# Looser waits at both ends, reordered weight preparation, and a shorter power of two in a fused Mamba-and-FFN kernel

## The chip, the cores and the metric

The kernel runs on one core of a Trainium2 chip. Its time is the device time of one execution in microseconds (us); the kernel before takes 1848.21 us, the median of three runs (1847.84 to 1850.84). Everything below comes from one profiled execution of it, which took 1849.32 us, of which 1847.5 us are the span that the trace covers.

## The reference, cut to what matters

For an input x of 2 x 2048 rows of 512 numbers the reference computes `x + attn(xn) + ffn(xn)`, where `xn` is the layer norm of x.

- `attn` is a Mamba-2 layer: `xn @ in_proj_w` gives z, x, B, C and dt; x goes through a causal convolution of four taps and a silu; a chunked state-space product with decays follows; the result is normed, scaled by `norm_scale` and `silu(z)` and multiplied by `out_proj_w`.
- `ffn` is a gated layer between Walsh-Hadamard transforms: `fwht(xn * SU_ug)`, then the products with `W_up` and `W_gate` (2048 x 512 each), `silu(gate) * up`, `fwht(. * SU_dp)`, and the product with `W_down` (512 x 2048), with scale vectors per row.

The transforms act on the activations in the reference; the kernel moves them onto the weights, once, ahead of the blocks.

## The kernel before, in words

The program has two parts. The **preparation** turns the weights into pairs of 16-bit tiles (a high part and a low rest) with power-of-two scales. The **blocks** then work through 16 blocks of 256 rows; every product with weights is three 16-bit products (high with high, high with low, low with high).

Every engine follows a list of step names written out by hand, in the preparation (`PREP_PE`, `PREP_ACT`, `PREP_DVE`, `PREP_SP`, lines 80 to 101) and in the blocks (`PE_STEPS` and the others). Each engine works its list strictly in order and waits in it on semaphores.

Steps of the preparation:

- **Loads (SP's list).** `nat0` to `nat7` are the eight groups of 512 rows of w_up and w_gate (1 MB each; `nat0` is loaded from ScalarE's queue at the very start). `dn0` and `dn2` are the two halves of w_down (2 MB each), `in` is in_proj (two loads of 2 MB and one of 288 KB), `wo1` is out_proj for its norms (2 MB), and `wo2` is out_proj again for its own preparation. `nat2` and later wait until group n-2 has been squared and mixed (lines 362 to 366).
- **Group of up or gate.** VectorE adds and subtracts halves (`bb`, lines 509 and 510, into `mixed`); ScalarE sums squares of the group's rows (`sq`, line 422); TensorE sums them over the partitions (`fs`, line 693, one product over four columns into bank 7), and VectorE (`fs`, lines 588 to 595) reduces the four, takes a power of two above the root (`power_above`) and its inverse, and scales the sign vector with it into `su_scale`. Four units per group follow: TensorE transposes four tiles (`T`, line 717), ScalarE copies them from the bank (`T`, line 437, into `wt`), TensorE multiplies with the Hadamard matrix (`H`, lines 728 and 729), ScalarE stores the high part with the group's scale (`H`, line 449), and VectorE stores the low rest (`H`, line 624). There are 32 such units, and 16 more of w_down.
- **w_down.** ScalarE scales its four rows of tiles (`dsc`, line 460) and squares them (`dsq`, line 464); VectorE mixes it in eight butterfly steps (`db`, lines 509 and 510 with 2048 columns; the digits are stage and half); T32 to T47 wait for all eight.
- **in_proj.** ScalarE squares pieces (`nq`, line 432), TensorE sums them (`nb`, line 700), VectorE takes maxima (`nb`), finds the scales (`ws`), and both store the pair (`wi`, lines 454 and 666).
- **Peaks (`pk`).** VectorE finds all remaining scales in some 10 us of small dependent steps with two exchanges with TensorE (lines 514 to 575). ScalarE's `pk` is only a wait for them. After it come out_proj (`wo`) and the units of w_down.
- **The first block's input.** VectorE norms it (`lna`, `lnb`, `lnc`), ScalarE and VectorE split it (`xh`, `xl`), and SP turns it with four DMA transposes (`turn_x`).

At the end of the preparation each of the five engines counts up `prepared`, and all wait there for 5 (lines 829, 894, 1016, 1154 and 1342). VectorE then drains, releases the ring's banks (line 1343) and clears the running state. TensorE's `bank` waits, for each ring product, until the bank's prior content has been read; for the first block this is line 1343's release.

In the blocks TensorE's list holds the FFN's gate and up products (`F0` to `F15`), its down products (`D`), the products of the state space (`xp`, `qk`, `cs`, `G`, `int`, `itr`, `st`, `z`) and out_proj (`O0`, `O1`); `D` and `O` collect in banks 6 and 7. All products go through the helper at line 910. SP's list loads the next block's input (`xin`), turns v, y and the next x (`td`, `yd`, `xd`), loads the residual (`res`) and stores the block before (`store`). In the last block `xin` loads block 0 again, and it is normed and turned for nothing. After the last block VectorE sums both halves (`final_sum`, line 1338) and SP stores 512 KB in one transfer (line 885).

Of the kernel before, what the change touches and what calls it, by code (L numbers as in the profile page):

```python
# [80 lines left out]
fs0 T0 T1 T2 H0 H1 T3 nb0 fs1 T4 H2 T5 H3 T6 T7 H4 H5 H6 T8 H7 T9 nb1 fs2 H8 T10 T11 nb2 H9 nb3 H10 H11 fs3  # L81
T12 nb4 T13 nb5 T14 H12 H13 T15 T16 fs4 T17 H14 H15 T18 T19 H16 H17 T20 H18 H19 T21 fs5 H20 H21 T22 T23 T24
H22 fs6 H23 T25 T26 H24 T27 H25 fs7 T28 H26 H27 T29 pk H28 T30 H29 T31 H30 H31 T32 T33 H32 T34 H33 T35 H34 T36
H35 T37 T38 H36 H37 T39 T40 H38 T41 H39 H40 T42 T43 H41 T44 T45 H42 H43 T46 H44 T47 H45 H46 H47
""".split()
PREP_ACT = """
sq0 nq0 dsc0 T0 T1 dsc1 sq1 T2 H0 dsc2 T3 H1 dsc3 dsq0 dsq1 T4 T5 H2 dsq2 dsq3 H3 H4 T6 T7 sq2 nq1 T8 T9 H5 H6
nq2 nq3 H7 T10 T11 sq3 H8 nq4 H9 nq5 H10 T12 T13 sq4 H11 H12 T14 T15 wi0 wi1 H13 T16 T17 H14 H15 wi2 wi3 T18
T19 sq5 H16 H17 T20 H18 T21 H19 sq6 T22 T23 H20 sq7 H21 T24 T25 H22 H23 H24 H25 T26 T27 H26 T28 H27 T29 T30
H28 H29 pk T31 wo0 wo1 wo2 H30 wo3 H31 wo4 wo5 T32 T33 wo6 T34 wo7 T35 H32 T36 H33 H34 T37 H35 H36 T38 H37 T39  # L90
T40 H38 T41 H39 T42 H40 T43 xh0 xh1 H41 T44 H42 T45 H43 T46 H44 T47 H45 H46 H47
""".split()
PREP_DVE = """
bb0 bb1 fs0 db00 H0 bb2 fs1 H1 nb0 db01 bb3 H2 db10 H3 H4 db11 fs2 nb1 H5 bb4 H6 nb2 H7 db20 nb3 fs3 H8 nb4 H9
H10 nb5 ws H11 bb5 H12 fs4 wi0 wi1 H13 H14 H15 wi2 wi3 db21 H16 H17 H18 H19 bb6 fs5 bb7 H20 db30 H21 fs6 H22
H23 H24 H25 fs7 pk H26 H27 db31 wo0 wo1 H28 H29 H30 wo2 H31 wo3 wo4 wo5 wo6 wo7 H32 H33 H34 H35 H36 lna H37
lnb lnc H38 H39 xl0 xl1 H40 H41 H42 H43 H44 H45 H46 H47
""".split()
PREP_SP = """
wo1 dn0 nat1 dn2 nat2 nat3 in nat4 nat5 nat6 nat7 wo2  # L100
# [40 lines left out]
def program(nc, u, in_w, conv_w, conv_b, a_log, dt_bias, d_param, norm_scale, out_w,  # L141
# [10 lines left out]
    with ctx:  # L152
# [115 lines left out]
        with ExitStack() as prep:  # L268
# [135 lines left out]
            def _(act):  # L404
# [9 lines left out]
                for step in PREP_ACT:  # L414
# [23 lines left out]
                    elif k == "H":  # L438
# [7 lines left out]
                        else:  # L446
                            a = n - UG_UNITS
                            dst, sc = wd[:, a, 0, :], down_store[:, a:a + 1]
# [17 lines left out]
                    elif k == "pk":  # L466
                        act.wait_ge(all_scales, 1)
                    elif k == "wo":
# [6 lines left out]
            def _(dve):  # L475
# [36 lines left out]
                def peaks():  # L512
# [7 lines left out]
                    power_above(rowpw[:, :], pw[:, :])  # L520
                    nc.vector.tensor_tensor(rowpw[:, :].rearrange("p (g t) -> p g t", g=8), cols[:, WS_UG:WS_UG + 32].rearrange("p (g t) -> p g t", g=8),
# [56 lines left out]
                for step in PREP_DVE:  # L578
# [100 lines left out]
            def _(pe):  # L679
# [7 lines left out]
                for step in PREP_PE:  # L687
                    k, n = parse(step)
                    if k == "fs":
# [3 lines left out]
                        nc.tensor.matmul(banks[7][:, 4 * n:4 * n + 4], ones[:, :], nsq[:, 4 * n:4 * n + 4], start=True, stop=True).then_inc(group_summed, 1)  # L693
# [126 lines left out]

        def position(step):
            return ring[RING.index(step) % BANKS]
# [5 lines left out]
        def _(sp):  # L828
            sp.wait_ge(prepared, 5)

            def body(i, following, first=False):
                for s in SP_STEPS:
                    k, at = kind(s), index(s)
                    if k == "store":
# [15 lines left out]
                    elif k == "xin":  # L850
# [3 lines left out]
                        sp.dma_start(xin[:, :, :], x_v[following]).then_inc(x_loaded, 16)  # L854
# [27 lines left out]
            for i in range(NBLOCKS):  # L882
                body(i, (i + 1) % NBLOCKS, first=i == 0)
            sp.wait_ge(out_ready, NBLOCKS * NT)
# [498 lines left out]
```

## Time and profile before

| | us |
|---|---|
| median of three runs | 1848.21 |
| profiled execution | 1849.32 |
| its span | 1847.5 |
| start of TensorE's first block product | 162.34 |
| TensorE busy, from 270 to 1740 us | 1470.00 |
| last product starts | 1836.87 |
| store leaves | 1844.23 |

Times in the rows are microseconds from the start of the span. PE is TensorE, PEld its weight loads, DVE VectorE, ACT ScalarE, POOL GpSimd, SPq and ACTq the queues from which DMAs are issued. "L509" is line 509 of the kernel. A bracket behind an instruction tells how long its engine was idle before it and whose event ended that; `<-issue` means that no wait was seen. A busy TensorE is not a TensorE at its peak, as its products are pipelined.

### The profile page before, as it was taken

How to read it: one execution, taken by the hardware profiler on the slowest of the kernel's cores; microseconds unless marked ns; L12 is line 12 of the kernel's file. 1: busy time of each engine (PE TensorE's matmuls, PEld its weight loads, DVE VectorE, ACT ScalarE, POOL GpSimd, SP SyncE). 2: the span in 40 equal slices, each digit the busy share in tenths (PEclk: the TensorE clock that was granted, in tenths of full speed). 3: DMA queues.
4: the chain of work that ended last, by engine and by line, in shares of the span. 5: the costliest groups of instructions: out<-in, count | busy, mean ns of one | idle time of the engine just before them, and what ended most of it. 6: DMA issues, size and time to landing. Idle time of an engine off the chain costs nothing.

```text
span 1847.5 us, 37420 instructions
## 1 busy us (share of the span) xinstructions
PE 1793.8 (97%) x13746; PEld 1241.9 (67%) x13746; DVE 1391.4 (75%) x2859; ACT 1223.8 (66%) x2582; POOL 306.4 (17%) x270
## 2 busy tenths in 40 slices
PE   4878999999999999999999999999999999999998
PEld 2336767676766768676766758677666757676675
DVE  6987867869586877868586877958676776858686
ACT  7967848576574848666584847666584857657483
POOL 0000212203030212203021221203021220303021
PEclk9999999999999999999999999999999999999999
DMA  8111223121312222131312322131322213121222
GB/s 326 69 69 47 58 58 81 32 81 39 81 47 61 78 47 76 41 79 41 89 47 58 81 44 76 36 78 47 85 53 58 81 34 74 43 81 47 64 75 58
DMA packets 217581, 125.74 MB, mean 68 GB/s; under 512 B 179662, under 2 KB 180790, under 8 KB 216886
## 3 DMA queue, kind: packets, MB, share of 16 engines
q1 hardware_dynamic: 216870, 122.30, 25.0%
q8 instruction: 109, 1.79, 0.4%
q10 hardware_dynamic: 528, 1.05, 0.2%
q14 instruction: 74, 0.61, 0.1%
HBM read 72.18 MB, written 8.65 MB: 44 GB/s over the span
## 4 chain that ended last, share of the span: by engine, by line
PE 90%; DVE 5%; DMA 1%; ACT 1%; issue 1%; SPq 1%; DVEq 1%; ACTq 0%
PE bank L910 88%; DMA big<-in_L_ffn_W_down_dram 1%; DVE wug L624 1%; DVE wi L666 1%; PE bank L728 1%; PE bank L729 0%; DVE big L509 0%; ACT big L460 0%; DVE wo L675 0%; SPq L873 0%; PE bank L717 0%; DVE wd L509 0%; DVE big L510 0%; ACT wi L464 0%; PE bank L732 0%
## 5 line engine op out<-in xcount | busy, mean ns | idle before, releaser
L910 PE MATMUL bank<-pair,wug 128*128 128x256 f16 x6144 | 699.8, 273 | 0.0
L910 PEld LDWEIGHTS bank<-pair,wug 128*128 128x128 f16 x6144 | 596.3, 98 | 90.3 <-issue 3.4
L910 PE MATMUL bank<-wd,h 128*128 128x512 f16 x1536 | 360.3, 379 | 0.0
L1183 POOL TENSOR_TENSOR state<-state,dec 128x512 f32<-128x512 f32 x64 | 84.2, 1325 | 1066.2 <-ACT neg L1098 805.4
L910 PEld LDWEIGHTS bank<-wd,h 128*128 128x128 f16 x1536 | 149.1, 98 | 160.5 <-DVE h L1241 0.2
L1230 DVE SCALAR_TENSOR_TENSOR pair<-pair,conv 128x256 f32<-128x256 f32 x384 | 193.2, 548 | 78.8 <-ACT pair L1046 68.9
L910 PE MATMUL bank<-wi,pair 128*128 128x512 f16 (+1 forms) x1152 | 201.6, 330 | 3.1 <-DVEq L1343 3.1
L910 PE MATMUL bank<-pair,wi 128*128 128x256 f16 x1536 | 172.9, 273 | 0.0
L1112 ACT ACTIVATE Mx<-Mx,cs_own 128x128 f32<-128x128 f32 x512 | 162.2, 388 | 8.2 <-DMA Mx<-cs_rows 7.6
L910 PEld LDWEIGHTS bank<-wi,pair 128*128 128x128 f16 x1152 | 101.5, 99 | 98.0 <-issue 3.9
L910 PEld LDWEIGHTS bank<-pair,wi 128*128 128x128 f16 x1536 | 149.9, 98 | 16.9
L1171 POOL TENSOR_TENSOR pair<-v 128x512 f32<-128x512 f16 x64 | 81.7, 1276 | 431.0 <-DMA v<-pair 385.9
L1263 DVE TENSOR_TENSOR Mx<-Mx,Gm 128x512 f32<-128x512 f32 x128 | 97.8, 764 | 32.7 <-ACT Mx L1116 23.5
L1061 ACT ACTIVATE pair<-bank,gate_scale 128x256 f32<-128x256 f32 x128 | 60.3, 471 | 91.5 <-PE bank L910 67.6
L1090 ACT ACTIVATE stateK<-state 128x512 f16<-128x512 f32 x64 | 39.7, 620 | 90.7 <-DVE state L1295 90.7
L1295 DVE SCALAR_TENSOR_TENSOR state<-bank,state 128x512 f32<-128x512 f32 x64 | 44.0, 688 | 73.5 <-PE bank L910 73.4
L1061 ACT ACTIVATE tg<-bank,gate_scale 128x256 f32<-128x256 f32 x128 | 59.8, 467 | 49.4 <-PE bank L910 48.5
L1237 DVE SCALAR_TENSOR_TENSOR tg<-tg,h_scale,bank 128x256 f32<-128x256 f32 x128 | 61.0, 476 | 37.7 <-ACT tg L1061 34.2
L1116 ACT ACTIVATE Mx<-Mx 128x512 f32<-128x512 f32 x128 | 80.6, 630 | 8.1
L910 PE MATMUL bank<-wo,Mx 128*128 128x512 f16 x384 | 85.5, 379 | 0.0
L910 PE MATMUL bank<-wo,yT 128*128 128x512 f16 x384 | 85.5, 379 | 0.0
L1268 DVE TENSOR_TENSOR Mx<-Mx 128x512 f16<-128x512 f32 x96 | 75.2, 783 | 12.7 <-ACT Mx L1127 10.6
(253 smaller groups left out, 2715.9 us busy)
## 6 DMA issues: line engine op xcount, KB each, us to landing
Mx<-cs_rows SPq DMA_DIRECT2D x128, 256.0 KB, 3.7
pair<-in_L_attn_u_dram SPq DMA_DIRECT2D x17, 512.0 KB, 3.6
Mx<-in_L_attn_u_dram SPq DMA_DIRECT2D x16, 512.0 KB, 3.8
out_dram<-Mx SPq DMA_DIRECT2D x16, 512.0 KB, 2.8
big<-in_L_ffn_W_down_dram SPq DMA_DIRECT2D x2, 2048.0 KB, 18.1
wug<-in_L_attn_in_proj_w_dram SPq DMA_DIRECT2D x2, 2048.0 KB, 13.4
pair<-in_L_ffn_W_gate_dram SPq DMA_DIRECT2D x4, 1024.0 KB, 5.3
pair<-in_L_ffn_W_up_dram SPq DMA_DIRECT2D x3, 1024.0 KB, 16.9
```

What stands on the lines that cost most here:

```text
L910: ins = nc.tensor.matmul(out, lhsT, rhs, start=first and n == 0, stop=last and n == len(pairs) - 1)
L1061: nc.scalar.activation(tg[c % 2][:, :], ug[c % 2][:, 0:TB], ACT.Silu, scale=gate_scale[:, c:c + 1]).then_inc(gate_ready, 1)
L1090: nc.scalar.activation(stateK[:, hf * 512:(hf + 1) * 512], state[:, hf * 512:(hf + 1) * 512], ACT.Copy, scale=1.0 / LOW).then_inc(state_hi ...
L1112: nc.scalar.activation(M[q][:, n, :], M[q][:, n, :], ACT.Relu, scale=-1.0, bias=cs_own[:, c, 4 * q + n:4 * q + n + 1])
L1116: nc.scalar.activation(M[q][:, :, :], M[q][:, :, :], ACT.Exp, scale=-1.0).then_inc(M_exp, 1)
L1171: pool.tensor_tensor(by_tile(vd[:, :]), v16[:, 4 * hf:4 * hf + 4, c, 0, :], v16[:, 4 * hf:4 * hf + 4, c, 1, :], ALU.add)
L1183: pool.tensor_tensor(half, half, bcast(dec3[:, 2, c, 8 * hf:8 * hf + 8], HD), ALU.mult).then_inc(state_faded, 1)
L1230: ins = nc.vector.scalar_tensor_tensor(cv[n % 2][:, c, :], x[:, c, j:j + TB], conv[:, CX * j + t:CX * j + t + 1], cv[n % 2][:, c, :], ALU. ...
L1237: nc.vector.scalar_tensor_tensor(tg[c % 2][:, :], tg[c % 2][:, :], h_scale[:, c:c + 1], ug[c % 2][:, TB:2 * TB], ALU.mult, ALU.mult).then_ ...
L1263: nc.vector.tensor_tensor(M[q][:, :, :], M[q][:, :, :], Gm[:, c, :].unsqueeze(1).to_broadcast([P, 4, P]), ALU.mult).then_inc(M_whole, 1)
L1268: nc.vector.tensor_tensor(M_lo[q], M[q][:, :, :], M_hi[q], ALU.subtract).then_inc(M_ready, 1)
L1295: nc.vector.scalar_tensor_tensor(half, o[:, :], 1.0 / PEAK, half, ALU.mult, ALU.add).then_inc(dve_emptied, 1)
```

## The change

- A group's power of two: TensorE adds the four columns itself (four products over one column into the same cell of bank 7), and VectorE shifts the exponent by 24 right and 23 left, takes the inverse as a multiply and add on the bits, and scales the signs. The power itself is taken back from the inverse for all groups at once in the peaks.
- New lists for TensorE, ScalarE, VectorE and SP. SP's now loads `dn0 nat1 dn2 nat2` ahead of `wo1` and `in`.
- ScalarE's `pk` wait goes; the wait for all scales stands in `wo` and in the units of w_down.
- TensorE waits at the start of the blocks for the split in_proj and the last copy (`wi_split`, `wt_copied`) in place of `prepared`; in the first block `bank` waits for the stores of the units only for banks 2 and 3, F0 and F1 wait for them, and `O` waits for the split out_proj.
- The last block loads, norms, splits and turns no further input. The last store is two stores, one for each half, and the final sum waits for the last down product only for the half that it closes.

```diff
 PREP_PE = """
...
+T0 T1 H0 T2 T3 H1 fs0 fs1 T4 H2 H3 T5 T6 H4 T7 H5 H6 T8 H7 T9 nb0 nb1 nb2 H8 T10 fs2 H9 T11 nb3 T12 H10 T13
+H11 nb4 T14 fs3 nb5 H12 T15 H13 T16 H14 H15 fs4 T17 T18 T19 H16 H17 T20 H18 H19 T21 fs5 T22 H20 H21 T23 T24
+H22 H23 T25 fs6 T26 H24 H25 T27 fs7 T28 H26 H27 T29 pk H28 H29 T30 T31 T32 H30 H31 T33 H32 T34 H33 T35 H34 T36
+T37 H35 H36 T38 T39 H37 T40 H38 T41 H39 H40 T42 H41 T43 T44 H42 T45 H43 H44 T46 H45 T47 H46 H47
 PREP_ACT = """
...
+T0 sq0 T1 dsc0 dsc1 dsq0 sq1 H0 T2 T3 H1 dsq1 dsc2 H2 dsc3 T4 T5 dsq2 H3 dsq3 T6 T7 H4 nq0 H5 nq1 T8 T9 nq2
+sq2 H6 nq3 nq4 H7 T10 H8 T11 H9 nq5 sq3 H10 T12 T13 H11 sq4 wi0 T14 T15 wi1 H12 H13 H14 T16 H15 T17 wi2 wi3
+T18 T19 sq5 H16 T20 T21 H17 H18 H19 H20 T22 T23 sq6 H21 T24 H22 T25 sq7 H23 H24 T26 T27 H25 H26 T28 T29 H27
+H28 H29 T30 T31 wo0 wo1 wo2 wo3 H30 wo4 T32 T33 wo5 wo6 T34 wo7 H31 T35 H32 T36 H33 H34 T37 T38 H35 H36 T39
+H37 T40 H38 T41 H39 T42 xh0 H40 T43 xh1 H41 T44 T45 H42 H43 T46 T47 H44 H45 H46 H47
 PREP_DVE = """
...
+bb0 db00 fs0 bb1 fs1 bb2 H0 H1 H2 db01 H3 db10 db11 nb0 bb3 H4 nb1 db20 H5 fs2 H6 nb2 db21 nb3 H7 H8 H9 bb4
+nb4 H10 fs3 nb5 ws bb5 H11 wi0 wi1 H12 H13 H14 fs4 H15 wi2 wi3 bb6 H16 fs5 H17 H18 H19 db30 bb7 H20 H21 fs6
+db31 H22 H23 H24 H25 fs7 pk H26 H27 wo0 H28 H29 wo1 wo2 H30 wo3 wo4 wo5 wo6 wo7 H31 H32 H33 H34 lna H35 H36
+H37 lnb lnc H38 xl0 H39 H40 xl1 H41 H42 H43 H44 H45 H46 H47
 PREP_SP = """
-wo1 dn0 nat1 dn2 nat2 nat3 in nat4 nat5 nat6 nat7 wo2
+dn0 nat1 dn2 nat2 wo1 in nat3 nat4 nat5 nat6 nat7 wo2
...
                     elif k == "fs":
-                        nc.vector.reduce_sum(fsq[:, g], banks[7][:, 4 * n:4 * n + 4], AX_X)
-                        dve.drain()
-                        power_above(fsq[:, g], fpw[:, g])
-                        inverse_power(fpw[:, g], fsq[:, g])
+                        nc.vector.tensor_scalar(fpw[:, g].bitcast(I32), banks[7][:, g].bitcast(I32), 24, 23, ALU.logical_shift_right, ALU.logical_shift_left)
+                        dve.drain()
+                        nc.vector.tensor_scalar(fsq[:, g].bitcast(I32), fpw[:, g].bitcast(I32), -1.0, float((254 - 65) << 23), ALU.mult, ALU.add)
+                        dve.drain()
...
-                        nc.tensor.matmul(banks[7][:, 4 * n:4 * n + 4], ones[:, :], nsq[:, 4 * n:4 * n + 4], start=True, stop=True).then_inc(group_summed, 1)
+                        for t in range(4):
+                            ins = nc.tensor.matmul(banks[7][:, n:n + 1], ones[:, :], nsq[:, 4 * n + t:4 * n + t + 1], start=t == 0, stop=t == 3)
+                        ins.then_inc(group_summed, 1)
...
-            sp.wait_ge(out_ready, NBLOCKS * NT)
-            sp.dma_start(out_v[NBLOCKS - 1], res[:, :, :]).then_inc(out_stored, 16)
...
+            for j in range(NT):
+                sp.wait_ge(out_ready, (NBLOCKS - 1) * NT + j + 1)
+                sp.dma_start(out_v[NBLOCKS - 1][:, j, :], res[:, j, :]).then_inc(out_stored, 16)
...
-            pe.wait_ge(prepared, 5)
+            pe.wait_ge(wi_split, 1)
+            pe.wait_ge(wt_copied, UNITS)
 
             def bank(i, s):
...
+                if ago > i:
+                    if RING.index(s) % BANKS >= 2:
+                        pe.wait_ge(hw_stored, UNITS)
+                    return position(s)
...
                     elif k == "F":
-                        pe.wait_ge(h_whole, (i + 1) * KF + c - 1)
+                        if i == 0 and c < 2:
+                            pe.wait_ge(hw_stored, UNITS)
+                        else:
+                            pe.wait_ge(h_whole, (i + 1) * KF + c - 1)
...
-                dve.wait_ge(h_used, (i + 1) * KF)
                 for j in range(NT):
+                    if down_closes(j):
+                        dve.wait_ge(h_used, (i + 1) * KF)
```

## Rows read from the trace of the kernel before

**Rows 1.** Windows: length, busy time (instructions) of each engine, granted clock, DMA share, GB/s.
```profile
22.28:160.77 138.49, 110.50 (x389) 55.65 (x389) 126.92 (x245) 112.88 (x208) 0.00 (x0) 0.96 0.31 108
8.90:107.90 99.00, 71.12 (x238) 35.86 (x239) 80.88 (x127) 87.83 (x166) 0.00 (x0) 0.95 0.46 175
...
162.34:165.06 2.72, 2.72 (x24) 2.72 (x25) 1.59 (x4) 0.00 (x0) 0.00 (x0) 0.50 0.02 6
270.00:1740.00 1470.00, 1470.00 (x11694) 1035.66 (x11692) 1101.72 (x2275) 962.27 (x2058) 265.37 (x224) 1.00 0.24 61
```

**Rows 2.** Waits of VectorE from 22.28 to 161 us: total, times, longest.
```profile
DVE wo L509 <- DMA pair<-in_L_ffn_W_up_dram: 13.5, 1, 13.5
...
DVE big L509 <- ACT wi L464: 0.3, 1, 0.3
```

**Rows 3.** Timeline of the opening: start, duration, engine, line, operation.
```profile
14.61 5.00 ACT L432 ACTIVATE wi<-wi,cols 128x512 bf16<-128x512 f32 x8 [2.63 <-DMA wi<-n_L_attn_out_proj_w_dram]
19.68 2.00 ACT L460 ACTIVATE big<-big,down_scale 128x2048 f32<-128x2048 f32 x1
...
22.28 1.22 DVE L509 TENSOR_TENSOR wo<-pair 128x1024 f32<-128x1024 f32 x1 [13.47 <-DMA pair<-in_L_ffn_W_up_dram]
...
26.04 2.29 DVE L509 TENSOR_TENSOR wd<-big 128x2048 f32<-128x2048 f32 x1
```

**Rows 4.** Timeline of one group's sum and power of two.
```profile
30.56 0.36 PE L693 MATMUL bank<-nsq,ones 128*128 128x4 f32 x2 [0.30 <-PE bank L700]
...
33.38 0.15 DVE L591 TENSOR_REDUCE fsq<-bank 128x1 f32<-128x4 f32 x1
...
34.53 0.23 DVE L595 TENSOR_SCALAR su_scale<-cols,fsq 128x4 f32<-128x4 f32 x1
```

**Rows 5.** Timeline: the last group's power of two begins.
```profile
115.71 0.15 DVE L591 TENSOR_REDUCE fsq<-bank 128x1 f32<-128x4 f32 x1
```

**Rows 6.** Timeline of the change from the preparation to the blocks.
```profile
157.65 1.26 SPq L266 DMA_TRANSPOSE pair<-pair  x1
...
158.63 2.14 DVE L624 SCALAR_TENSOR_TENSOR wd<-bank,down_store,wd 128x512 f16<-128x512 f32 x3 [0.55 <-ACT wd L449]
...
162.34 3.02 PE L910 MATMUL bank<-wi,pair 128*128 128x144 f16 x24 [3.09 <-DVEq L1343]
...
165.40 0.48 DVE L1201 TENSOR_SCALAR raw<-bank,scal 128x256 f32<-128x256 f32 x1 [1.09 <-PE bank L910]
...
169.41 0.18 DVE L1220 TENSOR_SCALAR pair<-pair 128x32 f32<-128x32 f32 x1
...
173.06 0.27 PE L954 MATMUL bank<-ident,kq 128*128 128x128 f32 x1
```

**Rows 7.** Timeline: two Hadamard products of TensorE after idle stretches.
```profile
97.44 2.08 PE L728 MATMUL bank<-wt,had 128*128 128x512 f32 x2 [3.51 <-DVE wug L624]
...
128.31 1.12 PE L728 MATMUL bank<-wt,had 128*128 128x512 f32 x2 [2.06 <-DVE wug L624]
```

**Rows 8.** Timeline of the end.
```profile
1833.11 1.90 SPq L265 DMA_TRANSPOSE pair<-pair  x1
...
1836.87 5.34 PE L910 MATMUL bank<-wo,Mx 128*128 128x512 f16 x24
...
1839.00 0.58 SPq L857 DMA_DIRECT2D Mx<-in_L_attn_u_dram  x1
1842.80 1.41 DVE L1338 SCALAR_TENSOR_TENSOR Mx<-bank,scal,Mx 128x512 f32<-128x512 f32 x2 [4.95 <-DMA Mx<-in_L_attn_u_dram]
1844.23 0.39 SPq L885 DMA_DIRECT2D out_dram<-Mx  x1
```

**Rows 9.** DMA issues of the whole span: count, KB each, median us to landing.
```profile
out_dram<-Mx SPq DMA_DIRECT2D x16, 512.0 KB, 2.8
...
pair<-pair SPq DMA_TRANSPOSE x68, 2.5
pair<-in_L_ffn_W_up_dram ACTq DMA_DIRECT2D x1, 1024.0 KB, 5.4
```

More of the change, by code:

```diff
@@ L447, in _ @@
                             a = n - UG_UNITS
+                            act.wait_ge(all_scales, 1)
                             dst, sc = wd[:, a, 0, :], down_store[:, a:a + 1]
@@ L520, in peaks @@
                     power_above(rowpw[:, :], pw[:, :])
+                    inverse_power(fsq[:, :], fpw[:, :])
                     nc.vector.tensor_tensor(rowpw[:, :].rearrange("p (g t) -> p g t", g=8), cols[:, WS_UG:WS_UG + 32].rearrange("p (g t) -> p g t", g=8),
@@ L819, in number, with down_closes @@
             return at[0] if len(at) == 1 else 10 * at[0] + at[1]
+        def down_closes(j):
+            return PE_STEPS.index(f"D{KF - 1}") > PE_STEPS.index(f"O{j}")
         def position(step):
@@ L829, in _, with body @@
             sp.wait_ge(prepared, 5)
-            def body(i, following, first=False):
+            def body(i, first=False, last=False):
                 for s in SP_STEPS:
                     k, at = kind(s), index(s)
+                    if last and k in ("xin", "xd"):
+                        continue
                     if k == "store":
@@ L853, in body @@
                         sp.wait_ge(v_turned[3], (i + 1) * 2 * 16)
-                        sp.dma_start(xin[:, :, :], x_v[following]).then_inc(x_loaded, 16)
+                        sp.dma_start(xin[:, :, :], x_v[i + 1]).then_inc(x_loaded, 16)
                     elif k == "res":
@@ L882, in _ @@
             for i in range(NBLOCKS):
-                body(i, (i + 1) % NBLOCKS, first=i == 0)
-            sp.wait_ge(out_ready, NBLOCKS * NT)
-            sp.dma_start(out_v[NBLOCKS - 1], res[:, :, :]).then_inc(out_stored, 16)
-            sp.wait_ge(x_loaded, 16 * (NBLOCKS + 1))
-            sp.wait_ge(out_stored, 16 * (NBLOCKS + 1))
-            sp.wait_ge(xT_loaded, 4 * 16 * (NBLOCKS + 1))
+                body(i, first=i == 0, last=i == NBLOCKS - 1)
+            for j in range(NT):
+                sp.wait_ge(out_ready, (NBLOCKS - 1) * NT + j + 1)
+                sp.dma_start(out_v[NBLOCKS - 1][:, j, :], res[:, j, :]).then_inc(out_stored, 16)
+            sp.wait_ge(out_stored, 16 * (NBLOCKS + 2))
         @block.tensor
@@ L901, in bank @@
                 return position(s)
-            def down_closes(j):
-                return PE_STEPS.index(f"D{KF - 1}") > PE_STEPS.index(f"O{j}")
             def products(out, pairs, first=True, last=True):
@@ L1003, in body @@
                         pe.wait_ge(yT_loaded[c], (i + 1) * 4 * 16)
+                        pe.wait_ge(wo_split, CX)
                         products(acc[c][:, :], [pq for a in range(CX) for pq in three(lambda u: yT[c][:, a, u, :], lambda u: wo[:, a, u, :])],
@@ L1143, in body @@
                         nc.scalar.activation(by_tile(y_hi[c][hf]), y[c][hf], ACT.Copy).then_inc(y_high, 1)
-                    elif k == "xh":
+                    elif k == "xh" and i < NBLOCKS - 1:
                         act.wait_ge(dve_emptied, (i + 1) * NR_DVE + emptied("itr11"))
@@ L1320, in body @@
                         nc.vector.tensor_tensor(by_tile(y_lo[c][hf]), y[c][hf], by_tile(y_hi[c][hf]), ALU.subtract).then_inc(y_split, 1)
-                    elif k == "xl":
+                    elif k == "xl" and i < NBLOCKS - 1:
                         low_xn(dve, i, at[0])
-                    elif k == "lna":
+                    elif k == "lna" and i < NBLOCKS - 1:
                         norm_sums(dve, i)
-                    elif k == "lnb":
+                    elif k == "lnb" and i < NBLOCKS - 1:
                         norm_root(dve)
-                    elif k == "lnc":
+                    elif k == "lnc" and i < NBLOCKS - 1:
                         norm_apply()
```

16 lines of the change are left out of this document (1 added, 15 removed).

## The prediction

> **What bounds the kernel now.** I read the windows by stage first. From 270 to 1740 us TensorE is busy 1470.00 of 1470.00 us at full granted clock [rows 1]: there the blocks cost what TensorE's products cost, and the change takes none of them out. So only two places can move: the preparation, before TensorE's first block product at 162.34 us [rows 6], and the tail after its last product, which ends at 1836.87 + 5.34 = 1842.21 us [rows 8].
>
> Next the waits of VectorE from its second group butterfly (22.28 us) to its last low half (158.63 + 2.14 = 160.77 us) [rows 3, 6]. The first row is 13.5 us for a load of w_up, which ends at 22.28; it and the last row are shown, and the six after the first sum to 3.8 us [rows 2]. So in those 138.5 us VectorE's queue stands still for 3.8 us and is taken for 134.7 us (busy 126.92, the rest are drains between dependent steps) [rows 1]. VectorE bounds the preparation; ScalarE (112.88) and TensorE (110.50) have room over the whole, but up to its last square sum at 107.9 us ScalarE is busy 87.83 of 99 us [rows 1]. It is the next bound.
>
> **The change, part by part.** The sum is made against the profiled execution: 1849.32 us, of which 1847.5 are span. It lies 1.1 us over the median of 1848.21; I take the gains off either.
>
> *The power of two in three steps.* Now a group's chain is six dependent VectorE steps; the first five start 0.23 us apart (33.38 to 34.53) [rows 4]. Reduce, add and one shift go: 3 x 0.23 = 0.69 us, for 8 groups 5.5 us. One more inverse, with its drain, comes into the peaks: 0.25 us. Net 5.3 us less on the bounding queue. TensorE gives back: the one product over 4 columns, two passes in 0.36 us [rows 4], becomes four such products over one column, so at most +1.08 us a group, 8.6 us in all. TensorE is free 28 of 138.5 us [rows 1], and the group chain (TensorE +1.08 at most, VectorE -0.69) grows by 0.4 us at most, so I cost it at nothing; with TensorE's room gone it costs up to 8.6.
>
> *New load order.* Now out_proj goes first and lands at 14.6, where ScalarE starts on it; the first half of w_down, queued behind it, lands at 19.68, and VectorE's first down butterfly comes at 26.04 [rows 3]. After, that half of w_down has the place of out_proj, and is as large (2 MB), so it lands near 14.6. ScalarE scales two rows (2.00 each [rows 3]) and VectorE begins its long run with that butterfly at about 14.6 + 4.0 = 18.6 us, not with w_up at 22.28. The next w_up group then arrives behind 3 MB and is hidden by the butterfly's 4.5 us. out_proj and in_proj come later by what passed them (3 MB, near 8 us), but ScalarE now takes their squares after the fourth row of w_down has been squared, at about 40 and 46 us in a walk through its new order; some 14 MB at the opening's pace are in at about 39. That cover is some 6 us; if it is gone, each us late is a us on ScalarE's early run.
>
> *New orders.* From 18.6 us VectorE has 134.7 - 5.5 + 0.25 = 129.4 us to do: its end would be 148.0 with no wait, 151.8 with the 3.8 us of now. Walking through the three lists with the durations of now, I find two new waits: about 1.7 us before the second half of the first down butterfly (ScalarE reaches the fourth row's scaling only at 33 us, behind a group's square sums), and 0 to 2 us of ScalarE's early run, which ends near 108 us as now. The last group's power is then found at about 113 us instead of 115.71 [rows 5], with a 4.4 us butterfly that came behind it already done ahead of it. So I take 5.5 us of waits: VectorE ends at 153.5, 7.3 us earlier. Bounds: 2 us of waits (most of today's gone, 150.0) and 10 (ScalarE or TensorE feeds it late, 158). The last unit steps (TensorE 13 transposes and products after VectorE's 31st low half) come out at about the same 153 us, so less than 150 is hard to get. ScalarE's wait for all scales moves to steps that need them: it was 4 us of idle ScalarE in a stretch where VectorE worked without pause; nothing.
>
> *TensorE's first wait.* Today TensorE starts 162.34 - 160.77 = 1.57 us after VectorE's last step: VectorE drains, joins the barrier, drains again and releases the banks. After, only the copies of the weights, the split in_proj and the turned x hold it. x's last transpose was issued at 157.65 and lands 2.5 us later [rows 6, 9], 160.15; in the new order VectorE's second low half of x stands one step nearer the end, so x lands at about VectorE's end. I take TensorE's start 0.2 us after it: 1.4 us gained (bounds 0.5 and 2.5). The banks of the last units are guarded in the third ring product and the first F, 3 to 5 us on, when VectorE is done. What is late next is VectorE itself: it still clears the state after the barrier, ready 3.55 us after its end (at 164.31, then 1.09 of wait for TensorE), and its chain to the decay inputs ends 4.2 us after the first bank is read (165.40 to 169.41 + 0.18), so at +7.8; TensorE asks for them 10.7 us after its start (173.06) [rows 6], or 9.5 with a fast first product. Covered by about 2 us.
>
> *The clock at the start.* The first product takes 2.72 us at granted 0.50, after 3.09 us of idle TensorE [rows 1, 6]. After a gap of 2.06 us a Hadamard product of two passes took 1.12, after one of 3.51 us 2.08 [rows 7]. The new gap is 1.5 (TensorE leaves before VectorE) + 0.2 = 1.7 us, nearer the first: then 24 products of 144 columns at full clock take near 1.5, saving 1.2 us (bounds 0 and 1.3). The Trainium skill (TensorE: Matmul & The Clock Gate, Part 1: The HAM clock gate) says that half rate is the idle state and that recent activity releases it; by it any restart from idle could be slow, and the sum would be 1.2 us higher. The trace agrees with it only for the longer gap.
>
> *The tail.* The last block skips the next block's load, norm and four transposes, so SP asks for the residual near 1833, where the first of those four stands now, not at 1839.00; it lands near 1837, under it TensorE's last product (1842.21). Today the residual lands at 1842.80, two sums run to 1844.21, and the store leaves at 1844.23 [rows 8]. After, the first half is summed and stored under the last product (its wait, D15, ends at 1837); the second starts at about 1842.27 and takes 0.73, its store leaves at 1843.03: 1.2 us gained. A store of 512 KB lands in 2.8 us; loads of 512 KB and 1 MB (3.8, 5.4 [rows 8, 9]) differ by 1.6, so half the bytes save at most 0.8 and at least 0: I take 0.4. Tail 1.6 us. What VectorE and ScalarE skip in the last block lies under TensorE and gives nothing, as do the added wait in O and the weaker wait in the final sum of the inner blocks.
>
> Sum: 7.3 + 1.4 + 1.2 + 1.6 = 11.5 us. Profiled 1837.8; median **1836.7**.
>
> **Rivals.**
> *A, VectorE unhindered.* Its waits shrink to 2 us (150.0), start and tail at their good ends: 10.8 + 2.5 + 1.2 + 2.0 = 16.5, 1831.7. For it: VectorE waits only 3.8 us now [rows 2]. Against: the unit chain at the end, and ScalarE's early run.
> *B, ScalarE and TensorE set the pace.* ScalarE gains only about 1 us by its fourth group's squares in my walk; if it and the unit chain hold VectorE to 10 us of waits, its end is 158: 2.8 + 1.4 + 1.2 + 1.6 = 7.0, 1841.2.
> *C, slower: TensorE falls to half clock and becomes the bound.* Its Hadamard product is 1.9 times as long cold [rows 7]. The 110.50 busy us of now were at a mean clock of 0.96 [rows 1]; at 0.75 they would be 141, with up to 8.6 us of extra sums some 149. With 19 us before its steady run TensorE ends near 168 and the body starts 6 us later than now, less 1.6 in the tail: about 1852. It becomes the bound at a mean clock under about 0.84 (126 + 8.6 + 19 = 153.6) and eats the whole gain under about 0.77. For it: six more passes per group, and a wait on VectorE of 3.51 us occurs now. Against: earlier data, fewer idle stretches.
> *D, the loosened start doesn't do it.* x, or something that this trace does not show, holds TensorE's start as now, and cold: 7.3 + 1.6 = 8.9, 1839.3.
>
> **How the numbers follow.** The forecast 0.50, A 0.15, B 0.20, C 0.05, D 0.10. Range 1831 to 1844: from A's end to beyond B; C and the poorer part of B stay out. The measurement tells 0.2% (3.7 us) from no change. Faster than 1844.5: the forecast, A, D and most of B, 0.87; within 0.2%: the tail of B with D added, 0.08; slower: C, 0.05.
>
> **What would show it.** The profile after should have: a VectorE group chain of three steps, near 0.6 us from first start to the next work; the first down butterfly near 18.6; VectorE's last low half near 153.5, with waits of about 5.5 us between; TensorE's first block product less than 0.5 us after that, in 1.5 us at clock near 1.0; no wait of TensorE before the transposes of q and k; the second half's sum 0.1 us behind the last product and the span's end about 4 us behind it instead of 5.3. A down load landing past 17 us, an end of VectorE past 158, or TensorE's clock under 0.8 in the preparation would make the prediction wrong.

## The result and the profile after

The changed kernel takes 1838.43 us (median of six runs, 1837.27 to 1839.65), the kernel before beside it 1849.01 (six runs, 1847.84 to 1850.84). The ratio is 0.9941, with a 95% interval of 0.9931 to 0.9951: some 11 us less. The profiled execution took 1837.27 us, of which 1835.6 are span; before it was 1847.5, so 11.9 us are to be found in the traces. It is the fastest of the six, 1.2 us under their median, and the medians differ by 10.6 us, so some 1 us of the 11.9 may be scatter. Four executions among the experiments below, two of them of the kernel before, took 4.9 to 10.8 ms and are left out of every figure.

The timeline of the opening, after (start, duration, engine, line, operation):

```profile
14.04 3.88 ACT L461 ACTIVATE big<-big,down_scale 128x2048 f32<-128x2048 f32 x2
...
17.96 2.29 DVE L509 TENSOR_TENSOR wd<-big 128x2048 f32<-128x2048 f32 x1 [9.15 <-ACT big L461]
...
21.04 0.95 PE L695 MATMUL bank<-nsq,ones 128*128 128x1 f32 x8
...
22.37 0.15 DVE L592 TENSOR_SCALAR fpw<-bank 128x1 int32<-128x1 int32 x1
22.60 0.15 DVE L594 TENSOR_SCALAR fsq<-fpw 128x1 int32<-128x1 int32 x1
22.83 0.23 DVE L596 TENSOR_SCALAR su_scale<-cols,fsq 128x4 f32<-128x4 f32 x1
22.97 1.22 DVE L509 TENSOR_TENSOR wo<-pair 128x1024 f32<-128x1024 f32 x1
```

ScalarE scales w_down at 14.04 where it squared out_proj before, and VectorE's first down butterfly comes at 17.96 instead of 26.04 [rows 3]. A group's power takes 0.60 us of VectorE (22.37 to 22.97). TensorE's sum now takes eight passes, 0.95 us, where two took 0.36 [rows 4]: some 0.6 us more a group.

Windows after (columns as in [rows 1]): VectorE's stretch, the first block product, and from the second product to the last product's end.

```profile
17.96:155.24 137.28, 112.95 (x460) 60.87 (x459) 123.69 (x222) 115.31 (x214) 0.00 (x0) 0.96 0.35 120
...
153.76:155.27 1.51, 1.51 (x24) 1.51 (x25) 1.48 (x3) 0.46 (x1) 0.00 (x0) 1.00 0.00 0
155.27:1832.31 1677.04, 1677.04 (x13323) 1180.61 (x13320) 1255.41 (x2578) 1097.50 (x2349) 302.24 (x256) 1.00 0.24 61
```

The body, 1677.04 us, is what it was: before, its second product began at 165.18 and its last one ended at 1842.21, 1677.03 apart. All of the gain lies at the two ends. The first product runs at granted clock 1.00 in 1.51 us, against 0.50 and 2.72 [rows 1]. (The granted clock is given as a share of full speed: 1.00 is TensorE's level of 2.4 GHz, 0.50 that of 1.2 GHz, and a value between them is a stretch with both.)

Waits of VectorE after, from its first down butterfly on (total, times, longest; the first row's 9.2 lies ahead of it):

```profile
DVE wd L509 <- ACT big L461: 10.3, 2, 9.2
DVE wd L625 <- ACT wd L450: 2.4, 4, 1.2
DVE fpw L592 <- PE bank L695: 1.2, 1, 1.2
DVE wug L625 <- ACT wug L450: 0.6, 1, 0.6
```

With the 1.1 us left of the first row and six rows of 0.3 to 0.6 that are not shown, these make about 7.7 us. The largest are the units of w_down at the end and one group sum on which VectorE stood.

The hand-over to the blocks, after:

```profile
147.93 0.68 DVE L255 SCALAR_TENSOR_TENSOR pair<-pair 128x512 f16<-128x512 f32 x1
...
149.88 1.41 DVE L625 SCALAR_TENSOR_TENSOR wd<-bank,down_store,wd 128x512 f16<-128x512 f32 x2 [0.60 <-ACT wd L450]
...
151.19 1.26 SPq L266 DMA_TRANSPOSE pair<-pair  x1
...
152.51 2.73 DVE L625 SCALAR_TENSOR_TENSOR wd<-bank,down_store,wd 128x512 f16<-128x512 f32 x4 [1.23 <-ACT wd L450]
153.76 1.67 PE L919 MATMUL bank<-wi,pair 128*128 128x144 f16 x24 [0.62 <-DMA pair<-pair]
...
162.88 0.18 DVE L1233 TENSOR_SCALAR pair<-pair 128x32 f32<-128x32 f32 x1
...
163.13 0.31 PE L966 MATMUL bank<-ident,kq 128*128 128x128 f32 x1
```

TensorE starts at 153.76, after 0.62 us of idleness that the last transpose of x ended (issued at 151.19), while VectorE works until 152.51 + 2.73 = 155.24. Before, it started 1.57 us after VectorE's last step; now 1.48 ahead of it. So VectorE's end no longer holds TensorE's start. The chain that ended last shows what does, in the same stretch (start, duration, what):

```profile
146.10 0.61 DVE pair L255
...
146.79 1.31 SPq L265
...
148.17 1.24 SPq L266
...
149.51 1.62 SPq L265
...
151.19 2.52 DMA pair<-pair
```

It runs from VectorE's first low half of x (L255) through SP, which issues the four transposes one after the other, to the landing of the last one at 153.71. VectorE's last low half of x starts at 147.93; its waits of 0.60 and 1.23 us at the units of w_down come after that and delay only VectorE itself.

At `qk` the decay inputs (162.88 + 0.18 = 163.06) come 0.07 us before TensorE asks for them: nothing is left of that cover.

The end, after:

```profile
1820.25 0.58 SPq L866 DMA_DIRECT2D Mx<-in_L_attn_u_dram  x1
...
1826.97 5.34 PE L919 MATMUL bank<-wo,Mx 128*128 128x512 f16 x24
1827.99 0.75 DVE L1352 SCALAR_TENSOR_TENSOR Mx<-bank,scal,Mx 128x512 f32<-128x512 f32 x1
1828.77 4.71 SPq L895 DMA_DIRECT2D out_dram<-Mx  x2
1832.36 0.75 DVE L1352 SCALAR_TENSOR_TENSOR Mx<-bank,scal,Mx 128x512 f32<-128x512 f32 x1 [3.62 <-PE bank L919]
```

The residual is asked for before the last product begins, half the result leaves under it, and the second sum starts 0.05 us behind the product's end (1832.31). The span ends 3.29 us behind that, against 5.29 before.

So: VectorE's end 160.77 - 155.24 = 5.53; TensorE's start against it 1.57 + 1.48 = 3.05; the first product 2.84 - 1.51 = 1.33 (start to start of the second); the tail 2.00. Together 11.9.

### The profile page after: what moved, and what is told of

Read it like the earlier page. It is cut to its first block, busy times and chain, and to the rows that moved or that the text cites. A ratio compares the mean times of both kernels' runs of the same rounds, so it can differ in the third digit from the quotient of the medians.

```text
span 1835.6 us, 37473 instructions
## 1 busy us (share of the span) xinstructions
PE 1796.7 (98%) x13794; PEld 1245.3 (68%) x13794; DVE 1385.1 (75%) x2816; ACT 1222.3 (67%) x2580; POOL 305.1 (17%) x270
## 3 DMA queue, kind: packets, MB, share of 16 engines
q10 hardware_dynamic: 528, 1.05, 0.2%
## 4 chain that ended last, share of the span: by engine, by line
PE 92%; DVE 4%; ACT 1%; issue 1%; DMA 1%; DVEq 1%; ACTq 0%; SPq 0%
PE bank L919 91%; DVE wug L625 1%; DVE wi L667 0%; DVE wo L509 0%; DVE big L509 0%; DVE wo L510 0%; ACT big L461 0%; DVE big L510 0%; DMA pair<-in_L_ffn_W_up_dram 0%; ACT dump L422 0%; ACT wi L465 0%; DVEq L610 0%; PE bank L731 0%; DMA pair<-in_L_attn_u_dram 0%; PE bank L966 0%
## 5 line engine op out<-in xcount | busy, mean ns | idle before, releaser
L1281 DVE TENSOR_TENSOR Mx<-Mx 128x512 f16<-128x512 f32 x96 | 76.4, 796 | 12.3 <-ACT Mx L1140 10.6
```

Source lines behind the costliest of these rows:

```text
L1281: nc.vector.tensor_tensor(M_lo[q], M[q][:, :, :], M_hi[q], ALU.subtract).then_inc(M_ready, 1)
```

## The experiments

Each was timed beside the kernel before, on the same chip; the rows come from several sessions and chips, so between rows ratios compare better than medians. "VectorE's end" is the end of its last low half, "start" TensorE's first block product, both in one profiled execution each. That end scatters by up to 1.1 us with the same preparation: 160.77 before and 159.68 with the new tail alone, 155.24 after, and 155.75, 155.61 and 156.19 with three variants that leave VectorE's part of the preparation alone (one store, old waits, old waits with busy TensorE).

| kernel | median us | ratio to before (95%) | VectorE's end | start |
|---|---|---|---|---|
| before | 1849.01 | | 160.77 | 162.34 |
| the change | 1838.43 | 0.9941 (0.9931 to 0.9951) | 155.24 | 153.76 |
| new tail alone | 1847.11 | 0.9990 (0.9981 to 0.9998) | 159.68 | 161.25 |
| change, old waits | 1842.30 | 0.9962 (0.9949 to 0.9974) | 155.61 | 157.18 |
| same, TensorE kept busy | 1840.37 | 0.9949 (0.9937 to 0.9962) | 156.19 | 157.76 |
| change, old power | 1843.09 | 0.9965 (0.9952 to 0.9977) | 161.27 | 159.35 |
| before, new power | 1849.38 | 0.9998 (0.9989 to 1.0007) | 162.47 | 164.05 |
| before, four steps | 1849.43 | 0.9996 (0.9987 to 1.0006) | 160.80 | 162.38 |
| before, longer sums | 1848.67 | 0.9995 (0.9986 to 1.0005) | 161.31 | 162.89 |
| change, old load order | 1843.38 | 0.9964 (0.9952 to 0.9977) | 160.85 | 159.91 |
| change, four steps | 1842.87 | 0.9963 (0.9950 to 0.9975) | 160.73 | 158.47 |
| change, one store | 1838.90 | 0.9943 (0.9930 to 0.9957) | 155.75 | 154.30 |
| short peaks | 1835.85 | 0.9927 (0.9913 to 0.9940) | 153.12 | 151.74 |
| short peaks, split last product | 1835.64 | 0.9927 (0.9914 to 0.9941) | 153.72 | 152.16 |

### The tail

**The new tail alone**, on the kernel before: the last block's skipped load, norm and transposes, the two stores, the later wait in the final sum.

```diff
+                    if last and k in ("xin", "xd"):
+                        continue
...
+            for j in range(NT):
+                sp.wait_ge(out_ready, (NBLOCKS - 1) * NT + j + 1)
+                sp.dma_start(out_v[NBLOCKS - 1][:, j, :], res[:, j, :]).then_inc(out_stored, 16)
```

> The kernel before with only the change at the end: the last block loads, norms and turns no further input, and the last store is two. Theory (the three places add up: start of the program, hand-over to the blocks, tail): TensorE's last product ends at 1842.2 us as before, the span ends 3.3 us behind it instead of 5.3, and the time falls by 2.0 us. Rival (the tail gives only what the earlier residual gives, 1.2 us, and the rest of the 2.0 seen in the changed kernel is something else): the span ends 4.1 us behind the last product, 1.2 us less. Rival (lighter last block lets TensorE end earlier): last product before 1841.5.

The span ended 3.25 us behind the last product: 2.0 us gained, and the ratio says 0.4 to 3.5. The last product ended at 1841.55, close to the bound of the second rival, but TensorE had also started 1.09 us earlier: from its start to that end it took 1680.30 us, against 1679.87 before. The lighter last block gave TensorE nothing.

**One store instead of two**, in the changed kernel:

```diff
-            for j in range(NT):
-                sp.wait_ge(out_ready, (NBLOCKS - 1) * NT + j + 1)
-                sp.dma_start(out_v[NBLOCKS - 1][:, j, :], res[:, j, :]).then_inc(out_stored, 16)
+            sp.wait_ge(out_ready, NBLOCKS * NT)
+            sp.dma_start(out_v[NBLOCKS - 1], res[:, :, :]).then_inc(out_stored, 16)
```

> The changed kernel with one last store of 512 KB after both sums instead of two of 256 KB. The span ended 3.29 us behind the last product there, 5.29 before the change. Theory (most of the tail's 2.0 us is the early residual, the smaller store gives the rest): the span ends 3.7 to 4.1 us behind the last product. Rival (what a store takes does not depend on its size): 3.3 us, as with two.

The last product ended at 1832.83 and the span at 1836.9, 4.07 us behind. Of the tail's 2.0 us the smaller store gives 0.8 and the early residual 1.2. This rests on the profiles: the medians differ by 0.5 us and the intervals of the ratios overlap.

### The hand-over

**The old waits at the start of the blocks**, in the changed kernel:

```diff
-            pe.wait_ge(wi_split, 1)
-            pe.wait_ge(wt_copied, UNITS)
+            pe.wait_ge(prepared, 5)
```

(and the guards of the banks, of F0 and F1 and of `O` with it).

> The changed kernel with TensorE's old wait at the start of the blocks: all five engines meet, and the banks are released after that. Theory: TensorE's first block product starts 1.6 us after VectorE's last low half (at about 156.8 us, 3.05 later than in the changed kernel), after more than 3 us of idle, so its first 24 products take 2.7 us at half clock instead of 1.5; together 4.2 to 4.4 us slower than the changed kernel, all of it seen at the end. Rival (the clock costs nothing, or the blocks take the delay in): 3.0 us slower or less. Rival (most of the gain was the wait, not the preparation): over 6 us slower.

**The same, with twelve throw-away products** ahead of TensorE's wait:

```diff
+            for _ in range(12):
+                nc.tensor.matmul(banks[7][:, 0:128], ones[:, :], ident[:, :], start=True, stop=True)
             pe.wait_ge(prepared, 5)
```

> The changed kernel with the old waits at the start of the blocks (as in the run that put them back, 1842.30 us), and twelve throw-away products on TensorE ahead of its wait for all engines, which fill part of its idle time. That run's first block product took 2.5 us after 3.7 us of idle TensorE. Theory (the long idle stretch is what costs the first product its speed): the first product takes 1.5 us at granted clock 1.0, the start comes as late as there, and the time is 1.0 to 1.3 us under that run's. Rival (the first product is slow because it waits for its data or for weight loads, whatever TensorE did before): still 2.5 us, time unchanged.

Timelines of TensorE's first two products, first with the old waits, then with the throw-away products:

```profile
157.18 2.69 PE L914 MATMUL bank<-wi,pair 128*128 128x144 f16 x24 [3.67 <-DVEq L1348]
159.66 6.06 PE L914 MATMUL bank<-pair,wi 128*128 128x256 f16 x48
```

```profile
157.76 1.66 PE L916 MATMUL bank<-wi,pair 128*128 128x144 f16 x24 [0.99 <-DVEq L1350]
159.26 5.40 PE L916 MATMUL bank<-pair,wi 128*128 128x256 f16 x48
```

The old waits cost 0.0021 of the time, 3.9 us, though the intervals of the two ratios overlap slightly; the profiles have 4.7 (3.05 of start against VectorE's end and 1.6 of clock). Both runs start 1.57 us after VectorE's end. After 3.67 us of idleness the first product lasts 2.48 us (start to start) at granted clock 0.58, and the second 0.66 longer; after 0.99 it lasts 1.50 at 1.00. That is 1.6 us for throw-away work, more than the 1.0 to 1.3 expected: the expectation had left out the second product. The medians differ by 1.9 us, but the intervals of the ratios overlap, so the size rests on the two profiles. The data and their wait were the same: it is the clock. By the Trainium skill (TensorE: Matmul & The Clock Gate, Part 1: The HAM clock gate) half rate is the state of an idle TensorE that activity lifts. The pair agrees: 0.58 behind the long gap, 1.00 behind the short one.

### The power of two and the orders

**The changed kernel with the old six-step power**, and **the kernel before with the new three-step power** (VectorE's `fs`, TensorE's `fs` and one line of the peaks exchanged whole, as the change's diff has them).

> The changed kernel with the old power of two: one product over four columns, then six dependent VectorE steps for each group, and no inverse in the peaks. Theory (VectorE's queue bounds the preparation): 8 x 0.69 - 0.25 = 5.3 us more on that queue; some of the 7.7 us that VectorE now waits there takes it in, so VectorE's last low half ends 3.5 to 5.3 us later than 155.2, and the time rises by as much (about 4). Rival (ScalarE and TensorE set the pace with the new lists): VectorE's end moves by under 1.5 us, and so does the time.

> The kernel before with only the new power of two, all lists, waits and the tail as before. Theory (VectorE's queue bounds the preparation, which waits only 3.8 us after 22.3 us): VectorE's last low half ends 4 to 5.3 us earlier than 160.77, and the time falls by 4 to 5. Rival (the lists were made for the old lengths, ScalarE's and TensorE's work fixes the steps): under 1.5 us. Rival (TensorE's four sums cost what VectorE gains): no change or slower.

The first came out as expected in the time, the second did not. In the new lists the old power costs 4.4 us (0.0024 of the time), and 6.0 us at VectorE's end, where at most 5.3 were expected; 1.5 us of these are a longer wait for the load of x (1.7 us instead of 0.3), which took 5.1 us in this run. In the old lists the new power brings nothing, and VectorE ends 1.7 us later, little more than the scatter. The chain that ended last, of this second kernel (start, duration, engine, what):

```profile
19.26 2.00 ACT big L460
...
46.54 0.98 ACTq L417
...
87.28 5.70 DVE wi L667 x8
93.07 2.29 DVE wd L509
```

and of the kernel before:

```profile
43.61 0.20 ACT wi L464
43.83 2.29 DVE big L509
...
78.96 5.59 DVE wi L666 x8
...
92.23 2.29 DVE wd L509
```

Before, the chain passes from ScalarE to VectorE at 43.8 and stays there past 92. With the short power it stays on ScalarE and TensorE until 87.28 and comes to the same butterfly (`wd L509`) at 93.07, not earlier than 92.23. That reads as two chains of about one length side by side: shortening one left the other. VectorE's waits show it too: [rows 2] summed to 3.8 us behind the first load, now they sum to 10.2:

```profile
DVE wo L509 <- PEq L724: 2.9, 2, 1.6
DVE wug L625 <- ACT wug L449: 1.8, 2, 1.2
```

Was it TensorE's longer sums? **The kernel before with four VectorE steps and the old product**, and **the kernel before with three more products at each sum** (ahead of the sum in the code, so that VectorE gets it later):

```diff
-                        power_above(fsq[:, g], fpw[:, g])
-                        inverse_power(fpw[:, g], fsq[:, g])
+                        nc.vector.tensor_scalar(fpw[:, g].bitcast(I32), fsq[:, g].bitcast(I32), 24, 23, ALU.logical_shift_right, ALU.logical_shift_left)
+                        dve.drain()
+                        nc.vector.tensor_scalar(fsq[:, g].bitcast(I32), fpw[:, g].bitcast(I32), -1.0, float((254 - 65) << 23), ALU.mult, ALU.add)
+                        dve.drain()
```

```diff
+                        for t in range(3):
+                            nc.tensor.matmul(banks[7][:, 40 + t:41 + t], ones[:, :], nsq[:, 4 * n + t:4 * n + t + 1], start=True, stop=True)
```

> The kernel before with a power of two in four VectorE steps, where TensorE's sum stays as it was: one product over four columns, two passes in 0.36 us. It has two steps fewer than before (0.46 us a group, 3.7 us for eight, less 0.25 us for one inverse more in the peaks). Theory T (the short chain brought nothing in the old lists because TensorE's four single-column products took 0.6 us more a group and stood in the way): VectorE's last low half ends at about 157.5 instead of 160.8, and the time falls by some 3 us. Theory S (in the old lists ScalarE's run of squares and copies, not VectorE's steps, sets when a group's power can be found, so VectorE only waits longer): VectorE ends within 1.2 us of 160.8, and the time is within 1.5 us of before.

> The kernel before with three single-column products more on TensorE behind each group's sum (their result is not used), VectorE's six steps as before. They take some 0.7 us a group. Theory T (TensorE's longer sums hold back the old lists): VectorE ends 2 to 6 us later than 160.8 and the time rises by as much. Theory S (ScalarE sets the pace, TensorE has room): VectorE ends within 1.2 us of 160.8 and the time is within 1.5 us of before.

It was not. Two steps fewer with TensorE's short sum: VectorE ends at 160.80, its waits rise from 3.8 to 7.7 us and eat the 3.4 saved. Longer sums alone: 161.31, no slower. TensorE's sums are free in the old lists, and so are VectorE's steps. That ScalarE's run, with the products between its steps, holds VectorE there is read from the chain above (from 46.5 to 87.3 us ScalarE is busy 38.18 of 40.80 with the short power); no run shortened ScalarE's work to test it.

**The changed kernel with four steps** asks the same in the new lists (TensorE's one product over four columns and VectorE's reduction back).

> The changed kernel with TensorE's one product over four columns and VectorE's reduction put back, the shorter power kept: four VectorE steps a group instead of three (8 x 0.23 = 1.8 us more on VectorE), TensorE some 0.6 us a group less. Theory (in the new lists VectorE's queue sets the end, TensorE has room for the four products): VectorE's last low half ends 1.3 to 2.5 us later than 155.24, and the time rises by as much over the changed kernel's. Rival (TensorE's four products stand in the same chain ahead of VectorE's steps and cost about what they save): VectorE ends within 0.7 us of 155.24, time unchanged.

VectorE ended 5.5 us later, and the time is 4 us longer by the ratios: the theory's side, but about twice its size. Up to the scales at the end of the peaks the delay is 2.3 us (`down_store` at 124.64 against 122.34), near what was expected. Then:

```profile
141.41 1.29 DVE L237 BATCH_NORM_STATS2 pair<-pair 128x6 f32<-128x512 f32 x2 [1.69 <-DMA pair<-in_L_attn_u_dram]
...
150.05 1.89 PE L735 MATMUL bank<-wt,had 128*128 128x512 f32 x2 [2.00 <-DVE wd L627]
...
152.59 2.43 PE L735 MATMUL bank<-wt,had 128*128 128x512 f32 x4
...
168.61 0.33 PE L966 MATMUL bank<-ident,kq 128*128 128x128 f32 x1 [0.62 <-DVE pair L1233]
```

The load of x took 5.0 us (136.38 to 141.4) instead of 3.6; TensorE then idled 2.00 us for a low half and ran at granted clock 0.55 in the 2.54 us from 150.05 and at 0.76 in the 2.31 us from 152.59. At `qk` it waited 0.62 us: the cover that was down to 0.07 is gone. In the run with the old power the load of x took 5.1 us, in the others 3.6 to 3.9 where VectorE waited for it. Why, no run tells. The fastest of the five executions, 1840.63 us, lies 2.2 us over the change's median, within what the theory had.

**The changed kernel with the old load order:**

```diff
-dn0 nat1 dn2 nat2 wo1 in nat3 nat4 nat5 nat6 nat7 wo2
+wo1 dn0 nat1 dn2 nat2 nat3 in nat4 nat5 nat6 nat7 wo2
```

> The changed kernel with the old order of loads: out_proj ahead of the first half of w_down, in_proj later. Theory (the early half of w_down is what lets VectorE start its long run at 18 us instead of 22): VectorE's first down butterfly comes at 23 to 26 us instead of 17.96 and VectorE, whose new list has it ahead of the first group's power, ends 4 to 7 us later than 155.2; the time rises by as much, to 1842 to 1845. Rival (the start does not matter, since the units at the end set VectorE's end): VectorE's waits at the end shrink instead and the time rises by under 1.5 us.

The opening of this run:

```profile
19.08 3.89 ACT L461 ACTIVATE big<-big,down_scale 128x2048 f32<-128x2048 f32 x2 [4.80 <-DMA big<-in_L_ffn_W_down_dram]
23.01 2.29 DVE L509 TENSOR_TENSOR wd<-big 128x2048 f32<-128x2048 f32 x1 [13.91 <-ACT big L461]
```

The butterfly comes 5.05 us later, VectorE ends 5.6 later, and the time is 0.0023 of before's longer, 4.3 us. So in the new lists taking back either the early w_down or the short power takes back about the whole gain of the preparation: they are not terms of a sum.

### A version that beats both

The chain of the changed kernel runs through the peaks: from 114.2 to 125.2 us nearly all of it is VectorE's small dependent steps, and behind them TensorE waited 1.31 us for a low half. **Short peaks**: maxima over rows ahead of the last group's power; three powers found together or earlier; the scales that only the blocks need moved to `ph` and `ps`, next to VectorE's waits.

```diff
-db31 H22 H23 H24 H25 fs7 pk H26 ... H33 H34 lna ... H42 H43 H44
+db31 H22 H23 pr H24 H25 fs7 pk H26 ... H33 H34 ph lna ... H42 H43 ps H44
...
-                    power_above(glob[:, 9:10], glob[:, 9:10])
-                    power_above(cmax[:, 6:7], cpw[:, 6:7])
+                    power_above(glob[:, 20:22], glob[:, 20:22])
```

> The changed kernel with the peaks treated as the group powers were: the maxima over rows come before the last group's power, three small powers are found together or earlier (some 1.6 us of dependent steps less), and the scales that only the blocks need (some 3 us of steps) are found later, in stretches where VectorE waited. Theory (these dependent steps stand on the chain that ends the preparation, VectorE's last low half of a gate unit let TensorE wait 1.31 us at 125.96): the scales for out_proj are there at about 120 instead of 122.7 us, TensorE's first block product starts 1.5 to 3 us earlier than 153.76, and the time falls by as much, to 1835.5 to 1837. Rival (TensorE's and ScalarE's 16 units of w_down set the end whatever VectorE does): the first product starts within 0.7 us of 153.76.

**The last out_proj product in two column halves** besides:

```diff
+                            products(acc[c][:, 0:256], pairs(slice(0, 256)), first=False, last=not down_closes(c)).then_inc(acc_filled, 1)
+                            products(ug[0][:, 0:256], pairs(slice(256, 512))).then_inc(acc_filled, 1)
```

> The version with the short peaks (1835.85 us), and in the last block the last out_proj product is made in two column halves of 256, the second in a free bank, so that all but the last 256 columns are summed and stored under it. Theory (the end is a last sum of 0.75 us and a store of 256 KB, both grow with size): the span ends 2.4 to 2.9 us behind the last product instead of 3.29, the time is 0.4 to 0.9 us under the short peaks', near 1835.3, and its ratio to before stays under that of the change (0.9941) by 0.001 to 0.002. Rival (48 products of 256 columns take longer than 24 of 512, or the third store queues): 3.3 us or more, no gain.

Rows of the short peaks: the scale that out_proj waits for, and TensorE's start.

```profile
119.94 0.22 DVE L549 TENSOR_SCALAR wo_store<-cols,glob 128x8 f32<-128x8 f32 x1
...
151.74 1.67 PE L926 MATMUL bank<-wi,pair 128*128 128x144 f16 x24 [1.11 <-DMA pair<-pair]
```

The scales are there at 120.2 instead of 122.7, and TensorE starts 2.0 us earlier, as the theory had it; x's transposes hold it, as in the changed kernel. The median is 2.6 us under the change's and the two sets of runs don't overlap, but the intervals of the ratios do, and the two were not timed side by side. The changed kernel with one store was, in the same session: its runs take 1838.47 to 1839.45 us, those of the short peaks 1835.45 to 1836.43. Of the 3.05 us between the medians the store explains 0.8 by the profiles; some 2.2 are left for the peaks. The split of the last product, by its timeline and its DMA issues (count, KB each, us to landing):

```profile
1825.82 5.40 PE L926 MATMUL bank<-wo,Mx 128*128 128x256 f16 x48
...
1831.27 0.48 DVE L1369 SCALAR_TENSOR_TENSOR Mx<-bank,scal,Mx 128x256 f32<-128x256 f32 x1 [1.87 <-PE bank L926]
```

```profile
out_dram<-Mx SPq DMA_DIRECT2D x15, 512.0 KB, 2.8
out_dram<-Mx SPq DMA_DIRECT2D x1, 256.0 KB, 2.0
out_dram<-Mx SPq DMA_DIRECT2D x2, 128.0 KB, 1.7
```

The span ends 2.7 us behind the product (1831.22 to 1833.9), 0.6 less than after the change; TensorE started 0.4 later in that run, and the median's 0.2 us is less than the runs can tell.

## Why the prediction was nearly right

**The bound and the places held.** The body kept its 1677 us; all came from the two ends, 11.9 us of span, or 10.6 by the medians, where the sum had 11.5.

**The preparation was mis-sized:** 7.3 us in the sum, 5.5 in the profile (4.5 if the ends of all runs with either preparation are averaged). The step that failed is "So I take 5.5 us of waits": 7.7 came. What VectorE has to do was right: 155.24 - 17.96 - 7.7 = 129.6 us occupied against 129.4. The first butterfly was 0.6 earlier than forecast (17.96), the last power later (114.00 against 113). The wait behind ScalarE's fourth scaling was there (1.1 us, forecast 1.7); the 2.4 us at the units of w_down (1.1 before) and the 1.2 us on the sum of the third group were not in the walk. Rival B was right in kind here: ScalarE and TensorE feed VectorE late, though by 2 us, not 5.

**The parts don't add, which the prediction did not see.** It gave the short power 5.3 us and found "two new waits" for the rest. By the crossed runs the power is worth 4.4 us (by the ratios) in the new lists and nothing in the old ones. The Trainium skill (VectorE: DVE Perf Modes, Rules for kernel authors) advises fewer instructions in a chain of dependent VectorE steps. In the new lists the runs agree, where VectorE's queue is the chain; in the old lists 24 fewer steps bought waits. The prediction called ScalarE "the next bound" from [rows 1], and that bound lay nearer than thought: by the chains of the old lists, at no distance at all.

**TensorE's first wait was worth 3.05 us, not 1.4,** because x did not land "at about VectorE's end" but 1.5 us before it, and TensorE is free to leave before VectorE. This miss and the preparation's (1.8 us the other way) are for the most part one. TensorE started at 153.76, where the sum puts it at 153.7. Of VectorE's 7.7 us of waits 1.83 (0.60 and 1.23) lie behind x's last low half; without them it would have ended at 153.4 (an estimate: 155.24 - 1.83), close to the 153.5 of the forecast. So the two terms were wrong and their sum, 8.6 against 8.7, was right. That the waits fell behind x and not ahead of it, where they would have cost time, was luck: the walk did not say so. Rival D (no help) falls with the old waits put back: they cost 3.9 us.

**The clock came as forecast, but not by its reason:** 1.33 us against 1.2, at 1.00, behind a gap of 0.62 us and not of 1.7. The step from "nearer the first" of two gaps to full clock is not safe: behind 2.06 us of idle time the clock was still full [rows 7], behind 2.00 us in the run with four steps it was 0.55. Rival C's slow TensorE did not come; its mechanism shows in small in that run.

**The cover at `qk` was over-counted:** "about 2 us" is 0.07, since TensorE starts ahead of VectorE. It cost nothing here, 0.62 us in the run with four steps and 0.27 in the version with the split last product.

**The tail:** 1.2 for the residual, as forecast; the smaller store 0.8, the upper of its bounds, where 0.4 was taken.

## What to carry to other kernels

Before pricing steps saved on the busiest engine, look for the second chain: follow what each engine's next step would wait for if those steps were gone, since two chains of one length give nothing when only one is shortened, and a reorder and a shorter chain may be worth something only together. At a hand-over let each engine wait for its own inputs and not for all engines; a long idle stretch that this saves may also save the slow clock behind it. Once a start is pulled ahead, recount every cover behind it from the new start.

## What the runs showed of the hardware

- Idle time of TensorE of 0.62, 0.99 and 1.16 us (the last with the old load order) ahead of the first block product, and of 2.06 us in the preparation [rows 7], left the granted clock at 1.00. Behind 2.00 us in the run with four steps it was 0.55 in the next 2.54 us. Behind 3.09 us it was 0.50 in the first product before and 0.68 with the new tail alone, behind 3.67 us 0.58; there the second product took 0.66 us more. So the length of a gap alone does not tell the clock behind it. Twelve throw-away products were worth 1.6 us.
- TensorE's sums of squares cost by passes: two over four columns took 0.28 to 0.36 us in seven of the eight groups before, eight over one column 0.95 to 1.05 in all eight after, so 0.12 to 0.18 us a pass with four columns or one.
- 512, 256 and 128 KB stored from SP's queue land in 2.8, 2.0 and 1.7 us.
- SP issues x's four transposes one after the other, at 1.24 to 1.62 us each, and the last lands 2.52 us after its issue begins.
- A load of 512 KB (x) took 3.6 to 3.9 us in most runs and 5.0 and 5.1 in two; the cause stays open.
